# ScalarE's order in the feed-forward step: two chunks of turned h copied ahead of x1's normalisation, four behind it

## What is computed

```
x = layernorm(x + attention(x))                    # x1
def fp4_linear(x, w):
    return einsum('bsk,nk->bsn', fp4_quant_dequant(x), fp4_quant_dequant(w))
h = silu(fp4_linear(x, w_gate)) * fp4_linear(x, w_up)
out = layernorm(x + fp4_linear(h, w_down))
```

## Time and profile before

| | us |
|---|---|
| median of 3 runs | 1951.57 (1950.83 to 1952.59) |
| the profiled execution, its own time | 1952.79 |
| span of its trace | 1950.9 |
| feed-forward, steady stage (1431.5 to 1824.1 of the span) | 392.6 |
| feed-forward, late tiles (1824.1 to 1910.0) | 85.9 |
| run-out (1910.0 to the end) | 40.9 |
| granted TensorE clock in all three | 1.00 |

### The profile page before, as it was taken

How to read it: one execution, slowest core, us unless ns; L and a number is a source line. 1 busy time by engine, 2 the same in 40 slices (tenths; PEclk the granted TensorE clock), 3 DMA queues, 4 the chain that set the end, 5 groups by cost and what they waited for, 6 DMA issues and landing times.

```text
span 1950.9 us, 43533 instructions
## 1 busy us (share of the span) xinstructions
PE 1917.4 (98%) x16042; PEld 1114.7 (57%) x16042; DVE 1829.3 (94%) x3088; ACT 1640.8 (84%) x3226; POOL 965.9 (50%) x833
## 2 busy tenths in 40 slices
PE   8999999999999999999999999999999999999998
PEld 7776444444444444444444444444478888888876
DVE  4798999999999999999999999998299999999997
ACT  5655999999999999999999999998967777777776
POOL 3000446675776765466232223323156666666785
PEclk9999999999999999999999999999999999999999
DMA  7985633455354445335444643543112211211210
GB/s 224 303 261 212 115 59 47 79 100 116 79 115 102 95 94 116 100 79 110 106 95 92 117 101 79 110 106 111 50 52 66 66 66 66 66 66 55 66 41 28
DMA packets 134976, 195.64 MB, mean 100 GB/s; under 512 B 38700, under 2 KB 83500, under 8 KB 134764
## 3 DMA queue, kind: packets, MB, share of 16 engines
q1 hardware_dynamic: 127084, 185.26, 38.4%
q10 hardware_dynamic: 7392, 7.34, 1.2%
q0 software_dynamic: 288, 0.27, 0.1%
HBM read 110.76 MB, written 80.48 MB: 98 GB/s over the span
## 4 chain that ended last, share of the span: by engine, by line
DVE 62%; PE 33%; issue 3%; ACT 1%; DMA 0%; DVEq 0%; SPq 0%; POOLq 0%; POOL 0%; ACTq 0%
DVE halfmax L1172 43%; DVE halfmax L1167 14%; PE ps L1478 10%; PE ps L1517 6%; PE ps L512 4%; PE ps L524 2%; PE ps L1082 2%; PE ps L1466 2%; PE ps L1489 2%; PE ps L1048 1%; PE ps L1534 1%; PE ps L499 1%; PE ps L1525 1%; DVE room L1668 1%; PE ps L1023 1%
## 5 line engine op out<-in xcount | busy, mean ns | idle before, releaser
L1133 ACT ACTIVATE room<-ps 128x512 f32<-128x512 f32 x2048 | 1086.2, 600 | 104.6 <-PE ps L1048 79.7
L1172 DVE TENSOR_REDUCE halfmax<-ps 128x1 f32<-128x512 f32 x1470 | 900.1, 674 | 0.0
L1048 PE MATMUL ps<-qs,ks 50*128 50x512 f32 x2048 | 718.9, 448 | 2.5 <-DVE halfmax L1172 1.2
L1023 PE MATMUL ps<-ks,qs 48*128 48x512 f32 x1960 | 678.4, 439 | 4.6
L1082 PE MATMUL ps<-room,vals 128*17 128x256 f32 (+2 forms) x8192 | 578.1, 384 | 0.2 <-ACT craw L1141 0.2
L1023 PEld LDWEIGHTS ps<-ks,qs 48*128 48x128 f32 x1960 | 311.4, 184 | 406.8 <-DVE halfmax L1172 250.0
L1048 PEld LDWEIGHTS ps<-qs,ks 50*128 50x128 f32 x2048 | 324.9, 184 | 19.5 <-ACT room L1133 13.8
L1082 PEld LDWEIGHTS ps<-room,vals 128*17 128x17 f32 x8192 | 167.4, 96 | 251.2 <-issue 186.7
L164 POOL CAST mrow<-turned_rows 128x32 fp32r<-128x32 f32 x32 | 6.7, 208 | 605.7 <-DVE turned_rows L159 605.7
L1167 DVE TENSOR_REDUCE halfmax<-ps 128x2 f32<-128x1024 f32 x245 | 295.2, 1205 | 0.9 <-PE ps L1023 0.8
L1478 PE MATMUL ps<-wguT,xqT 128*128 128x512 f32 (+1 forms) x1152 | 266.4, 384 | 4.2 <-DVE xqT L1708 4.2
(11 more groups left out here) (129 smaller groups left out, 2316.5 us busy)
## 6 DMA issues: line engine op xcount, KB each, us to landing
qk_parts<-parts SPq DMA_DIRECT2D x64, 512.0 KB, 4.8
qs<-qk_parts SPq DMA_DIRECT2D x192, 128.0 KB, 4.3
ks<-qk_parts SPq DMA_DIRECT2D x192, 128.0 KB, 6.7
ctx_raw<-craw SPq DMA_DIRECT2D x64, 256.0 KB
ready<-passing_half SPq DMA_DIRECT2D x27, 512.0 KB, 5.0
pairs<-ready SPq DMA_DIRECT2D x27, 512.0 KB, 3.6
out_dram<-fin SPq DMA_DIRECT2D x64, 128.0 KB, 1.7
passing<-ctx_raw SPq DMA_DIRECT2D x58, 128.0 KB
```

Of the source, the lines that this page charges most:

```text
L1023: nc.tensor.matmul(ps[:, MX + max_number(i, u, bank) % 4, :], qs[rows, i.slot(RING), pair, t * P:(t + 1) * P], ks[rows, i.slot(RING), pair ...
L1048: nc.tensor.matmul(ps[:, score_bank(i, s, n), :], ks[rows, slot, pair, kt * P:(kt + 1) * P], qs[rows, slot, pair, qh * BANK:(qh + 1) * BAN ...
L1133: nc.scalar.activation(prob[:, prob_slot(i, s), score_order(i, s)[n], :], ps[:, score_bank(i, s, n), :], ACT.Exp, scale=float(D) ** -0.5). ...
L1172: nc.vector.tensor_reduce(halfmax[:, i.slot(2), bank, column:column + 1], ps[:, at + bank, :], AX.X, ALU.max, negate=True).then_inc(max_re ...
```

## The change

ScalarE's list for a step is cut finer. `x1_normal` becomes `x1_shift` (the two tiny instructions) and `x1_normal` (the normalisation alone); `copy_hT` keeps the copies of chunks 4 and 5, and `copy_rest` is the copy of chunks 0 to 3. The new order is `x1_shift`, `copy_hT`, `x1_normal`, `copy_rest`. No instruction, size or semaphore is added or removed.

```
-        def x1_normal(t):
+        def x1_shift(t):
             due(act, "rstd1_ready", t.lin(1, 1))
             shift(t, 0, 0, "shift1_chain")
 
+        def x1_normal(t):
             due(act, "z_used", t.lin(1, 1 - U))
             nc.scalar.activation(x1[:, t.slot(U)], y[:, :], ACT.Identity, bias=centre[:, 0, 1:2],
                                  scale=rstd[:, 0, 1:2]).then_inc(sems["x1_ready"], 1)
...
             nc.scalar.activation(hT[rows, 5, :], ps[rows, HT + 1, P:2 * P],
                                  ACT.Copy).then_inc(sems["hT_ready"], 1)
+
+        def copy_rest(t):
             act.wait_ge(sems["hT_psum"], t.lin(2, 2))
             nc.scalar.activation(hT[:, 0:4, :].rearrange("p c n -> p (c n)"), ps[:, HT, :],
                                  ACT.Copy).then_inc(sems["hT_ready"], 1)
...
-            for lag, stage in ((3, copy_xqT), (9, output), (2, bend_x), (4, bend_h), (3, silu), (1, x1_normal),
-                               (5, copy_hT)):
+            for lag, stage in ((3, copy_xqT), (9, output), (2, bend_x), (4, bend_h), (3, silu), (1, x1_shift),
+                               (5, copy_hT), (1, x1_normal), (5, copy_rest)):
```

## The result

The changed kernel takes 1954.93 us (median of 15 runs, 1953.17 to 1957.51) against 1951.90 of the kernel before in the same series (15 runs). The ratio is 1.0014, 95% interval 1.0007 to 1.0020: 3.0 us slower, where 1.7 us faster was forecast. The profiled execution took 1955.01, its span is 1952.7.

The account below looks back on a forecast made before the run. TensorE's order was taken to set the pace, VectorE's in the late tiles. 24 periods x 0.07 = 1.7 us saved, from 1951.57 to 1949.9 us, range 1947.6 to 1953.0.

Parts of the forecast that it names:

- The 24 waits ahead of L1534: TensorE's weight loads waiting for bank 3, once a period, 5.2 us in total; the change was to remove them.
- late next: Chunks 0 to 3's copy holds the odd step's chunk-0 load, leaving 0.07 of the 0.24 offered there.
- x1 later: x1's normalisation ends 0.31 later in even, 0.56 in odd steps; VectorE's own list covers this at no cost.
- The new wait for h's transposes: Ahead of ScalarE's copies of chunks 4 and 5: ScalarE now waits a little for TensorE, holding x1 and chunks 0 to 3.
- d: Delay from the end of h's second transpose to ScalarE's copy, derived from the run-out as 0.06.
- e: Extra cost of the condition ahead of chunk 4's copy beyond d; 0 in the forecast, up to 0.07 allowed.
- Same: Verdict that the time changes by less than about 0.2% (3.9 us), given chance 0.84.
- B: Rival: the new wait on ScalarE cancels the gain; 0.06 a period lost, 1953.0 us; chance 0.24, shared with a no-effect rival.
- L1591 still stands behind all the same work: ScalarE's copy of chunks 0 to 3: reordered slots 0.26 + 0.30 + 0.51 keep their sum, so it comes no earlier.
- Does L1591 move with a faster TensorE? I think not.: In the odd step chunks 0 to 3 hang on a rigid loop through three engines, whose only slack is 0.07.
- C: Rival: the wait for h's transposes holds ScalarE's list longer; e = 0.2 would give 7.7 us slower, 1959.3; chance 0.04.
- A: Rival: chunks 0 to 3 gate nothing, the whole wait returns; 7.9 us less, 1943.7; chance 0.12, including partly over 3.9.

Follow-up runs that it names:

- x1_last: The changed kernel with x1's normalisation moved behind all copies, chunks 0 to 3 included: 1944.91 us against 1951.94 before, ratio 0.9958.
- new_order_own_wait: The changed kernel with the wait for the shift's second instruction moved from chunk 4's copy to x1's normalisation: 1953.07 us against 1952.11 before.
- new_order_rows0: The changed kernel with odd tiles' chunk 5 copy on rows 0 to 63 (result not the reference's): 1945.52 us against 1951.94 before.
- new_order_even_only: The changed order only in ScalarE's steps that copy an even tile, the old order for odd tiles: 1950.21 us against 1951.94 before.
- old_order_chunk5_by_pair: The kernel before with chunk 5 of two tiles turned and copied once, in the odd step, over 128 rows: 1947.13 us against 1950.65 before.
- new_order_chunk5_first: The changed kernel with chunk 5 copied before chunk 4: 1948.30 us against 1952.11 before, ratio 0.9979.

## Why the prediction was wrong

**What held.** The 24 waits ahead of L1534 went; chunks 0 to 3 were "late next", and their load is what TensorE waits for now. The even step saved about what was said (0.06 to 0.07 of 0.09). x1 later costs VectorE nothing: x1_last delays it twice as far and is 7.0 us faster than before. The late tiles are as good as unchanged (VectorE 83.64 of 85.90, before 84.18). The new wait for h's transposes is real: L1588 starts 0.09 behind the end of chunk 5's transpose (1700.67), where d = 0.06 was said, so e was 0.03; new_order_own_wait gives back 0.05 a period. The chunk-0 loads of the odd steps were to be held about 0.2; they are held 0.54. "Same" (a difference under 3.9) came out too, but with the sign against it and beyond B's 1953.0, so that is luck and not the working.

**The step that failed.** "L1591 still stands behind all the same work: slots 0.26 + 0.30 + 0.51 in a new order, the sum unchanged." The sum was not invariant. From the start of chunk 4's copy to the start of chunks 0 to 3 it is 1.21 instead of 1.07: 0.28 + 0.30 + 0.63. The slot of an instruction is not its own; it depends on what stands beside it. L1572's 0.51 was read where chunk 4's copy followed it and held 0.09 of overlap. Placed directly behind a copy on rows 64 to 127, it doesn't hand that overlap on. This 0.12 and the 0.02 ahead of chunk 5, with e = 0.03, make 0.17; the prediction had the odd step's path 0.02 longer than before, and 0.02 + 0.17 = 0.19 is what the odd step shown lost (0.21 in the median). Of the overlap, new_order_rows0 shows that the rows are the cause: with the offset gone, all three starts overlap and the time falls 6.4 us below before, not 3 above.

The rows had shown it in advance: in the earlier trace rows L1588 starts 0.01 behind L1587's end and L1591 0.03 behind L1588's, while L1587 starts 0.09 before L1572's end. The two late starts were taken as fixed slots.

**The second error.** "Does L1591 move with a faster TensorE? I think not." It does. new_order_even_only kept its saving (16.28 against 16.33); there was room, since `silu` of the odd step had been held by TensorE's gate product by some 0.05. A delay that passes through the earlier trace rows says that the chain can't absorb it; it doesn't say that the chain could not come earlier. That there is a limit further on, the traces suggest and don't prove: at shorter periods `silu` of the odd step falls back towards L1489 and follows L1610 with the full overlap (0.71 ahead at 16.07 in new_order_rows0, 0.64 at 16.16 in old_order_chunk5_by_pair, medians of 23). What limits those kernels was not taken apart. This error alone would have made the forecast too cautious, with the sign right; the even step's saving and the odd step's loss simply add: 24 x (0.19 - 0.06) = 3.1.

**The rivals.** B and C named the right place, L1591 late in ScalarE's list, and the wrong cause. The price e of the wait was 0.03 and could not have done it: with e = 0.03 the prediction's formula still gives a gain, 0.07 - 0.02 - 0.03 = 0.02 a period. It was the missing overlap, which stood in no rival. A was right in that the odd step can move: x1_last, at 7.0 below before, has most of A's 7.9.

**What stays open.** Why the loss reaches the start of chunks 0 to 3 behind x1 in the changed kernel, while it ends after one start with chunk 5 first and in x1_last (L1573 starts 0.11 before L1594's end). Pointer operands are excluded. That x1 reads another memory than its neighbours was not tried. Whether the start row counts in the source (PSUM) or in the target (SBUF) is open too: new_order_rows0 changed both. The wait's own share and that of the gap also weren't separated beyond new_order_own_wait.

## What to carry to other kernels

Before moving an instruction, look whether it starts before or after its predecessor's recorded end, and do so for each neighbour pair that the move creates; durations and slots from the old order don't add up in a new one. When a wait goes, the next one behind it is the forecast's real subject, and a step with no idle time in front may still follow another engine: compare its distance to that engine's events in two steps. Where a copy must start on row 64, put it where the engine waits anyway, ahead of its full-height neighbours (as new_order_chunk5_first does), or gather two halves into one copy.

## What the runs showed of the hardware that was not expected

A 64-row ScalarE copy from PSUM that starts on row 64 starts only behind its predecessor's recorded end (by about 0.01), and its successor 0.01 to 0.03 behind its own end; on rows 0 to 63 both overlap by 0.10 (new_order_rows0 against the changed kernel). In the changed kernel the start after that is late as well. Per pair of tiles this is 0.12 in the old order and 0.40 in the changed one.
